# Query and key projections of the first attention as three products of split operands

## What is computed

```
x = _layernorm(x)
q = jnp.einsum('bse,hde->bhsd', x, Wq) + bq[None, :, None, :]      # 16 heads of 64
k = jnp.einsum('bse,hde->bhsd', x, Wk) + bk[None, :, None, :]
v = jnp.einsum('bse,hde->bhsd', x, Wv) + bv[None, :, None, :]
scores = jnp.einsum('bhsd,bhtd->bhst', q, k) / scale               # causal
att = jax.nn.softmax(scores, axis=-1) / scale
z = jnp.einsum('bhst,bhtd->bhsd', att, v)
x = x + z.reshape(b, s, h * dh) @ proj
```

## Time and profile before

| | |
|---|---|
| device time, median of 3 runs | 1182.9 us (1182.59 to 1183.47) |
| profiled execution | 1174.82 us, its span 1173.0 us |
| mean granted TensorE clock of the profiled execution | 0.956 of full speed |
| busy PE, DVE, ACT, POOL | 91%, 66%, 61%, 46% of the span |
| first attention's loop | from about 41 us to about 607 us of the span |
| its steady units | one each 34.7 us |

### The profile page before, as it was taken

The page is one execution under the profiler, slowest core; times in us unless marked ns, Lnnn a source line. Parts: engine busy times, 40 slices in busy tenths (PEclk is TensorE's granted clock), DMA queues, the critical chain, the costliest instruction groups (busy, mean ns, idle before and its releaser), DMA issues.

```text
span 1173.0 us, 16993 instructions
## 1 busy us (share of the span) xinstructions
PE 1071.4 (91%) x5839; PEld 584.6 (50%) x5839; DVE 770.1 (66%) x1547; ACT 719.8 (61%) x1173; POOL 541.1 (46%) x446
## 2 busy tenths in 40 slices
PE   4699999999999999999956799999999579999998
PEld 2445555455455545555536422222322258778876
DVE  5767877777787777777545322225221379999998
ACT  4345555555565565555422499998999466666663
POOL 1356666666656666666630000000000126788786
PEclk9789999999999999999976699999999879999999
DMA  4111111111111111110200000000000002112110
GB/s 123 27 26 37 43 33 37 43 32 31 44 43 26 44 43 26 37 44 20 64 0 1 3 8 12 12 12 9 10 11 10 10 0 93 58 69 76 67 54 37
DMA packets 35290, 40.30 MB, mean 34 GB/s; under 512 B 19652, under 2 KB 22484, under 8 KB 34188
## 3 DMA queue, kind: packets, MB, share of 16 engines
q1 hardware_dynamic: 35212, 39.30, 13.0%
HBM read 19.23 MB, written 1.11 MB: 17 GB/s over the span
## 4 chain that ended last, share of the span: by engine, by line
PE 59%; DVE 27%; issue 9%; SPq 1%; ACT 1%; POOL 1%; DMA 1%; DVEq 0%; ACTq 0%; POOLq 0%
PE banks L1003 10%; PE banks L400 8%; PE banks L991 6%; PE banks L345 5%; PE banks L385 5%; DVE qb L1308 5%; PE banks L321 5%; PE banks L386 4%; PE banks L421 3%; PE banks L366 3%; DVE kb L581 2%; DVE banks L601 2%; DVE qa L581 2%; DVE zz L630 2%; DVE qb L610 2%
## 5 line engine op out<-in xcount | busy, mean ns | idle before, releaser
L710 POOL TENSOR_TENSOR pacc<-pacc,prob 128x1024 f32<-128x1024 f32 (+3 forms) x160 | 274.0, 1712 | 64.4 <-ACT prob L512 55.1
L1012 ACT ACTIVATE prob<-banks 128x1024 f32<-128x1024 f32 x256 | 238.7, 1094 | 22.1 <-PE banks L991 22.1
L512 ACT ACTIVATE prob<-banks 128x512 f32<-128x512 f32 (+3 forms) x384 | 167.8, 488 | 113.4 <-PE banks L386 111.8
L1341 POOL TENSOR_TENSOR ka<-prob,qb 128x512 fp32r<-128x512 f32 x108 | 165.0, 1549 | 59.6 <-ACT qb L1291 33.1
L385 PE MATMUL banks<-qa,ka 128*128 128x512 f32 (+3 forms) x384 | 150.7, 400 | 1.3 <-ACT prob L512 1.3
L400 PE MATMUL banks<-prob,v 128*64 128x512 f32 (+3 forms) x768 | 145.0, 498 | 1.0 <-POOL prob L701 1.0
L1297 ACT ACTIVATE prob<-banks,w 128x512 f32<-128x512 f32 x144 | 94.7, 687 | 71.3 <-PE banks L1259 71.3
L1003 PE MATMUL banks<-prob,v 128*32 128x512 f32 x1024 | 137.1, 608 | 0.8 <-DVE pacc L1020 0.3
L386 PE MATMUL banks<-qb,kb 72*128 72x512 f32 (+3 forms) x384 | 131.5, 350 | 0.0
L957 POOL TENSOR_TENSOR sq<-sq 64x512 f32<-64x512 f32 x8 | 8.3, 1033 | 261.3 <-DVE sq L953 261.3
L701 POOL TENSOR_SCALAR_AFFINE_SELECT prob<-prob 128x256 f32<-128x256 f32 x128 | 52.1, 407 | 147.6 <-ACT prob L512 145.9
(11 more groups left out here) (211 smaller groups left out, 1610.7 us busy)
## 6 DMA issues: line engine op xcount, KB each, us to landing
qb<-qa SPq DMA_DIRECT2D x64, 128.0 KB, 2.3
ka<-ka SPq DMA_DIRECT2D x64, 128.0 KB, 2.3
prob<-gate_rows SPq DMA_DIRECT2D x8, 1024.0 KB, 4.7
w<-in_experts SPq DMA_DIRECT2D x9, 514.0 KB, 3.5
wqkv<-in_wqkv SPq DMA_DIRECT2D x16, 193.0 KB, 2.4
x<-in_x SPq DMA_DIRECT2D x4, 256.0 KB, 4.1
zz<-pacc SPq DMA_DIRECT2D x64, 16.0 KB
wpr<-pacc SPq DMA_DIRECT2D x64, 16.0 KB
```

Source lines behind the costliest of these rows:

```text
L512: act.activation(pr[:, j % NRING, h, 0:wd], banks[:, h, 0:wd], ACT.Exp, scale=SCALE0).then_inc(s_exp, 1)
L710: pool.tensor_tensor(pacc[:, sbk, :, o:BLK], pacc[:, sbk, :, o:BLK], pr[:, j % NRING, :, 0:wd], ALU.add).then_inc(s_padd, 1)
L1012: act.activation(prob[:, n % NP1, :], banks[:, 2 * (n % 3):2 * (n % 3) + 2, :].rearrange("p b c -> p (b c)"), ACT.Exp, scale=2 * SCALE1).t ...
L1341: pool.tensor_tensor(act2[1][:, tb % 2, i, :], hid[:, tb % 2, i, :], act2[0][:, tb % 2, i, :], ALU.subtract).then_inc(s_hlP, 1)
```

## The change

x after the first layer norm, and the query and key weights, are each split into an fp32r head and the fp32r rest. `qk_pe` then makes each projection as three fp32r products (head by head, head of the weights by rest of x, rest of the weights by head of x) into one PSUM bank, in place of one fp32 product.

The weights are split on Pool, with one copy and one subtraction of 128x256 each, in step 9 of unit u for unit u + 2; those of units 0 and 1 ahead of the loop. x is split once: the heads of its first 1024 tokens by ACT beside its copy to `xT`, their rests by DVE, the other 1024 tokens by Pool ahead of the loop. PE gets a wait for the split weights at i = 0, in unit 0 also for the rests of x, and in unit 8 for those that Pool made. To make room in SBUF, small tiles of later stages are laid over tiles that are free by then. The value projection stays as it was.

```diff
@@ ln_act
                 act.wait_ge(s["turned"], i + 1)
+                if k == 0 and i < 2:
+                    act.activation(xhi[:, i * BLK:(i + 1) * BLK], banks[:, i, :], ACT.Copy).then_inc(s_xhi, 1)
                 act.activation(xT[:, i * BLK:(i + 1) * BLK], banks[:, i, :], ACT.Copy).then_inc(s["xT"], 1)
@@ qk_pe
-            pe.matmul(banks[:, qk_bank(n, i), :], wqkv[:, w, isk * D:(isk + 1) * D],
-                      xT[:, b * SEQ + half * BLK:b * SEQ + (half + 1) * BLK], start=True, stop=True).then_inc(s_qk, 1)
+            if i == 0:
+                pe.wait_ge(s_whl, 2 * (n + 1))
+            if n == 0 and not isk:
+                pe.wait_ge(s_xlo, half + 1)
+            elif n == PAIRS and i == 0:
+                pe.wait_ge(s_xloP, 2)
+            c, wc = slice(b * SEQ + half * BLK, b * SEQ + (half + 1) * BLK), slice(isk * D, (isk + 1) * D)
+            for k, (wk_, xk) in enumerate(((0, xhi), (0, xlo), (1, xhi))):
+                mm = pe.matmul(banks[:, qk_bank(n, i), :], whl[:, w, wk_, wc], xk[:, c], start=(k == 0), stop=(k == 2))
+            mm.then_inc(s_qk, 1)
+
+        def wsplit_pool(pool, n, w):
+            pool.wait_ge(s_wq[w], 8 * (n - w) + 16)
+            if n > 1:
+                pool.wait_ge(s_qk, 4 * (n - 1))
+            pool.tensor_copy(whl[:, w, 0, :], wqkv[:, w, 0:2 * D]).then_inc(s_whl, 1)
+            pool.wait_ge(s_whl, 2 * n + 1)
+            pool.tensor_tensor(whl[:, w, 1, :], wqkv[:, w, 0:2 * D], whl[:, w, 0, :], ALU.subtract).then_inc(s_whl, 1)
+
+        def xsplit0_pool(pool):
+            for i in (2, 3):
+                c = slice(i * BLK, (i + 1) * BLK)
+                pool.wait_ge(ln[0]["xT"], i + 1)
+                pool.tensor_copy(xhi[:, c], xT[:, c]).then_inc(s_xhiP, 1)
+                pool.wait_ge(s_xhiP, i - 1)
+                pool.tensor_tensor(xlo[:, c], xT[:, c], xhi[:, c], ALU.subtract).then_inc(s_xloP, 1)
+
+        def xsplit0_dve(dve):
+            for i in (0, 1):
+                c = slice(i * BLK, (i + 1) * BLK)
+                dve.wait_ge(s_xhi, i + 1)
+                dve.wait_ge(ln[0]["xT"], i + 1)
+                dve.tensor_tensor(xlo[:, c], xT[:, c], xhi[:, c], ALU.subtract).then_inc(s_xlo, 1)
@@ unit0_pool
             for j in range(12):
                 sbk, t, o, wd = slot_of(j)
                 k = masked(j)
+                if j == 9 and u < 2 * PAIRS - 2:
+                    wsplit_pool(pool, u + 2, w)
                 pool.wait_ge(s_exp, 2 * (12 * u + j + 1))
@@ gpsimd
             pool.wait_ge(s_setup, N_SETUP)
+            wsplit_pool(pool, 0, 0)
+            wsplit_pool(pool, 1, 1)
+            xsplit0_pool(pool)
             units0(pool, unit0_pool)
@@ vector
             ln_dve(dve, 0, lambda e, n: e.wait_ge(s_x[n // 4], 16) if n % 4 == 0 else None)
+            xsplit0_dve(dve)
             dve.wait_ge(s_const, 16)
             dve.tensor_copy(msk[:, BLK - P:BLK], cst[:, C_MS:C_MS + P]).then_inc(s_setup, 1)
```

More of the change, by code:

```diff
@@ L137, in build_kernel @@
         small = sb("small", [P, PROJ + NE0 * PROJ + 1])
-        dn = sb("dn", [P, NT, DALL])
-        pj = sb("pj", [P, NT, PROJ])
+        dn = prob[:, 0, 0:NT * DALL].rearrange("p (n k) -> p n k", n=NT)
+        pj = prob[:, 1, 0:NT * PROJ].rearrange("p (n k) -> p n k", n=NT)
         sq = zero[:, :].rearrange("p (n k) -> p n k", n=NT)
@@ L164, in build_kernel @@
         qv = v[:, :, :, :].rearrange("p b t (h j) -> p b t h j", j=32)
-        sq1 = sb("sq1", [2 * GH * DK, BLK])
+        sq1 = wqkv[0:2 * GH * DK, :, :].rearrange("p w c -> p (w c)")[:, 0:BLK]
         zs = pacc
@@ L175, in build_kernel @@
         rT = pacc[0:RH + 1, :, :, :].rearrange("p k h c -> p (k h c)")
+        xhi = sb("xhi", [P, TOK], F32R)
+        xlo = sb("xlo", [P, TOK], F32R)
+        whl = sb("whl", [P, 2, 2, 2 * D], F32R)
         gl = sb("gl", [P, NT, NE1])
[L177 to L180, removed]
+        ga = wkT[:, :].rearrange("p (n e) -> p n e", e=NE1)
+        oh1 = wvT[:, :].rearrange("p (n e) -> p n e", e=NE1)
+        oh2 = woT[:, :].rearrange("p (n e) -> p n e", e=NE1)
+        gw = a1[:, :].rearrange("p (n e) -> p n e", e=NE1)
         gT = v[:, 0, 0:4, :].rearrange("p t d -> p (t d)")
@@ L206, in build_kernel @@
         s_qk, s_hi0, s_lo0, s_vp, s_v = (sem(n) for n in ("qk_projected", "qk_hi_done", "qk_lo_done", "v_projected", "v_stored"))
+        s_xhi, s_xlo, s_whl = sem("x0_rounded"), sem("x0_split"), sem("qk_weights_split")
+        s_xhiP, s_xloP = sem("x0_second_rounded"), sem("x0_second_split")
         s_dup = [sem(f"{n}_copied") for n in ("q_first", "k_first", "q_second", "k_second")]
```

## The result

The changed kernel takes 1166.86 us (median of 16 runs, 1165.53 to 1175.12); the kernel before, run beside it again, takes 1175.5 us (16 runs, 1173.3 to 1183.92). The ratio is 0.9919 with an interval of 0.99 to 0.9938, so the change makes the kernel faster by 0.8%. The forecast time was 1175.3 us: 8.4 us too high, and the range missed the result by 2.6 us at its lower end (1169.5). The gain it was built on was nearly right: forecast 7.6 us, measured 7.3 us between the two profiled executions (spans 1173.0 and 1165.7; forecast 1165.4). Of the 7.3, 6.3 us lie between the first and the last output projection of the first attention (508.19 us before, 501.90 after). Most of the rest, 1.1 us, lies behind it, where nothing was changed; over all profiles here that part takes 566.0 to 569.4 us.

A forecast was written before the change was run, and what follows sets the result against it. TensorE was taken to bound the kernel (59% of the chain, DVE 27%). Gains of 0.17 + 0.36 = 0.53 us over 15 units, 7.95, less 0.3 at the start, took 7.6 off 1182.9: 1175.3 us, range 1169.5 to 1179.3.

The forecast's parts named there:

- the baseline: Time the gain was taken off: the median of 1182.9 us, not the profiled execution's 1174.82 us.
- Place A: First half's q and k projections, step 1: gains 0.17 us a unit, not 0.36, as the turn waits for DVE's last maximum.
- Place B: Second half's projections, step 7: keeps the full product saving of 0.36 us a unit (low end 0.28).
- Pool: Weight split in step 9: adds 1.2 us on Pool, hidden with 0.9 us slack before TensorE needs the mask; costs nothing.
- Ahead of the loop: Before the loop: ACT's six copies instead of four delay what follows by 0.3 us (0.15 to 0.45).
- (1): Unit 0: race tips so DVE's product precedes Pool's sum, saving 2.2 us, with the clock 3.4 more; chance 0.22.
- (2): Second half's gain eaten by DVE or ACT in a wait taken as slack; 2.3 us gain left, 1180.6 us; chance 0.12.
- (3): Pool's split delays the mask of step 9, deciding from a 2.1 us insertion; slower from 2.8 us; chance 0.06.
- A worse fall of the clock: Stages after: a lower clock, standing for the rest of the slower side; grouped with (3), chance 0.06.
- Faster: Whole kernel: faster by over 0.2%, chance 0.82, from 0.60 for the worked-out forecast plus 0.22 for (1).

The follow-up runs named there:

- e4: Changed kernel with all splitting kept but every projection an fp32 product again: 1176.6 us, ratio 1.0003 to the kernel before.
- e3: Changed kernel with only the first half's projections (Place A) as three products, the second half's in fp32: 1174.21 us, ratio 0.998 to the kernel before.
- e2: Changed kernel with only the second half's projections (Place B) as three products, the first half's in fp32: 1167.77 us, ratio 0.9924 to the kernel before.
- e5: Changed kernel with the subtraction of the weights done once more on Pool: 1166.61 us, ratio 0.9918 to the kernel before.
- e6: Changed kernel with three more subtractions of the weights on Pool: 1188.75 us, ratio 1.0108 to the kernel before.
- e1: The changed kernel again without any edit, for a second profile: 1167.46 us, ratio 0.9938 to the kernel before.
- e8: Changed kernel with ACT's roundings behind its four copies of x and DVE's rests behind its mask copy: 1166.76 us, ratio 0.9927 to the kernel before.
- e7: Changed kernel; in unit 0, Pool's step-5 sum waits for DVE's two 128x128 products: 1163.55 us, ratio 0.9884 to the kernel before.
- e9: Kernel before, without the split, with the wait of e7 added on Pool in unit 0: 1175.04 us, ratio 0.9973 to the unedited kernel before.
- e10: Changed kernel with both edits, of e7 and e8: 1165.95 us, ratio 0.9927 to the kernel before.

## Why the prediction went as it did

**What failed is the baseline.** The step is "the difference lies outside what I change, so I take the gain off the median: 1175.3 us". The profiled execution took 1174.82 us and three others 1182.9; I read the 8 us as something that would stay. The difference does lie outside the change, as far as e4's profile stands for such an execution (it has it ahead of the first output projection and at the last distance but one; no execution of before from the highest group was profiled), but it comes and goes between executions: most of the runs of before are near the profiled one, and its median over 34 is 1175.3. The same 7.6 us taken off the profiled execution is 1167.2, against 1166.86. The range failed with it: it held the unknown costs of the change and none of the baseline, though the 8 us stood in the data.

**Place A** was right. Forecast 0.17, measured 0.16 (0.14 alone in e3), by the reason given: the turn waits for the last maximum (start of the last run of maxima to turn: 2.09 us, forecast 2.08), and e2, with the old product at A, has the turn 0.21 us behind that maximum and no wait. But the wait is only part of why A gives 0.15 us less than B: 0.09 of it stood there before the change (1.82 against 1.91), where both now take 1.26 or 1.27 us from the first to the last product, and 0.07 is the longer distance to the turn (0.40 against 0.33). So taken by B's 0.33, TensorE had about 0.23 us to give at A and not the 0.36 of the forecast.

**Place B** was right in kind and 0.05 too large: forecast 0.36, measured 0.31. I had 0.226 us for a product, from a run of twelve; inside this row the starts stand 0.2325 apart ((274.60 - 273.67) / 4), which for six is 0.04 of it. The first stands 0.34 ahead of the second, which my 0.19 of other costs had covered. Per unit this makes 0.47 where the sum had 0.53, and over 15 units 7.0 instead of 7.95 us. The medians differ by 8.6 us; no run tells where the 1.6 us beyond the units come from.

**Pool** was right: copy 0.39 (taken 0.26 to 0.40), subtraction 0.73, insertion 1.16 against 1.2, slack 1.05 against 0.9, and e5 and e6 confirm the point from which it would have decided. e4 puts its whole price at 0.02 us a unit.

**Ahead of the loop** was wrong in size: forecast +0.3 (0.15 to 0.45), shown by e1 0.04. ACT had a gap of 0.26 us ahead of its copies; in e1 six in a row start 0.48 to 0.56 us apart, where I had taken 0.54 to 0.60, and end at 16.07, as the four ended at 16.03. Even these 0.04 us are the shift of the first copy (12.91 against 12.87). So the forecast gain and the measured one agree partly because two terms were off in opposite ways (0.9 us too much gain in the loop, 0.3 us too much cost ahead of it), and partly by chance, since the profiles differ by more than that in stretches that nobody changed.

**The rivals.** (1), the race: in the changed kernel's two profiles the pair still starts within 0.01 us and Pool wins, as in e4, e5, e6 and e8. It did tip in e2 and e3, and gave what the rival's own caveat said, next to nothing, since Pool then cuts in ahead of the second product. The 2.2 us exist (e7, e9), but it takes a wait to have them. (2), the gain at B eaten: fell with e2. (3), the mask of step 9: a true mechanism out of reach (e6). A worse fall of the clock in the stages behind did not come: from 600 to 1160 us its mean is 0.93 in both profiles.

**Faster** had 0.82, which was right.

## What to carry to other kernels

A sum made on one profiled execution belongs on that execution's time; where its time and the median of the runs shown differ by as much as the gain, the range has to hold both. Splitting an fp32 product into three fp32r products pays on TensorE by the distances of the starts in the target row (here 6 x 0.2325 us against 4 x 0.43), and the splitting costs next to nothing (here 0.02 us a unit) on an engine with slack, which the next consumer of that queue bounds (here 2.2 us) and not the engine's busy share. Look for a two-input VectorE instruction that starts together with a Pool instruction and is waited for: one wait on Pool shortened TensorE's wait by 2.2 us here, with or without the change. In the time that is 0.3% in the kernel before, with an interval of 0.07 to 0.47%; in the changed kernel e7 shows about as much and e10 none that is clear.

## What the runs showed of the hardware

- TensorE's level differs from one execution to the next of the same program: the sixteen bias products ahead of the loop took 1.92 us in e1 and 3.60 in after, and the trace's first clock record, of full speed, starts at 15.66 and 19.62 us. Over all kernels here that record starts between 14.3 and 28.0 us, and the windows show 1.00 ahead of it whatever the level was. Together with the last distance but one between output projections (34.0 or 37.1 us, granted clock 1.00 or 0.93 from 540 to 590 us) and unit 0 it accounts for the 8.6 us by which e4's profiled execution is longer than that of before, more than the change. What chooses is open. Whether the level in unit 0 returns sooner with a shorter wait is open too: 0.87 in e7, 0.74 in e9 and e10 at the same wait of 2.8 us.
- A DVE product of 128x128 with two SBUF inputs takes 2.48 us if Pool's sum of 128x1024 wins the start, 0.29 us otherwise; with starts within 0.01 us either wins. Two 128x512 subtractions take 1.03 and 1.75 us beside Pool's split of x (e8), and 0.69 us each alone.
- Pool's subtraction of 128x256 takes 0.73 us in one half of the double buffer and 0.64 us in the other (seen in e3, e4 and e6). No run tells why.
